# A deep attention layer whose rotary products are taken from PSUM by DVE, with POOL adding them and the FFN's next front a third earlier

## The chip, the cores and the metric

The kernel runs as one program on one core of a Trainium2 chip (trn2). The time is device time in microseconds, from the start to the end of an execution; several executions are given by their median. The engines are PE (TensorE), DVE (VectorE), ACT (ScalarE), POOL (GpSimd) and SP (SyncE, which only issues DMAs here).

## What is computed

Sixteen sequences of 256 rows with 128 channels go through four residual stages with layer norms. The change concerns the last one, a stack of six layers, each with a local attention and an FFN. Cut to what matters:

```python
def attn_layer(x, Wqkv, qs, ksc, Wo):            # x: (16, 256, 128), 16 heads of 64
    q, k, v = split(x @ Wqkv, 3)
    q = l2norm(q) * qs; k = l2norm(k) * ksc      # norm per row and head
    q = q * cos * scale + rotate_half(q) * sin * scale
    k = k * cos / scale + rotate_half(k) * sin / scale
    out = local_attention(q, k, v)               # windows of 32 rows, each looks at itself and the one before
    return out @ Wo

def ffn_layer(x, g, bln, W1, b1, W2, b2):
    a, gate = split(layernorm(x, g, bln) @ W1 + b1, 2)
    return a * gelu(gate) @ W2 + b2

for i in range(6):
    x = attn_layer(shift_tokens(x), ...) + x
    x = ffn_layer(shift_tokens(x), ...) + x
```

## The kernel before

All rows lie in SBUF as `X` (128 partitions, 32 blocks of 128 rows). The deep stage is written as one instruction stream for each engine, with semaphores between them. A sequence `n` is two blocks (`k`). Its work is put into 16 steps by hand-written tables (`PROJ_STEPS`, `SINE_STEPS`, `NORM_STEPS` and so on); `heads(n)` runs steps 0 to 15 of sequence `n`, steps 16 to 29 of `n - 1`, and the projection steps -16 to -1 of `n + 2` beside them. On every engine a step's order is: the attention's part first (`attend`), then the projection of `n + 2`, then what is left of `n + 1`. The streams loop over pairs of sequences (`Fori`), with the first and last ones of a layer written out.

The projection of a sequence has 13 slots: slot 0 turns the two blocks of X, slots 1 to 8 are the q and k products (k, part, half of 512 columns), slots 9 to 12 the four V products. A product is three matmuls (`split_product`, high and low parts). They go through two PSUM banks, `gen0` and `aux`, in turn. In the attention steps V slots of sequence `n + 1` stand between the q/k slots of `n + 2`: PE's order is slots 1, 2, 3, 4, V 9, V 10, 5, 6, 7, 8, V 11, V 12.

After a product, ACT copies the bank to `raw` (L1588) and squares it into `sq` (L1592), both inside the SBUF tile that the profile calls `spare`; then the bank is free (`proj_drained`). POOL multiplies the swapped halves by the sine table into `t2` (L1993, also `spare`), DVE multiplies `raw` by the cosine table in place (L1754), adds the two (L1761) and sums the squares per head (L1748). After the four quarters DVE works out the inverse norms by three Newton steps (L1767 to L1782), and POOL multiplies `raw` by them (L2003). PE turns the result (L1366), ACT keeps it in `qT` and `kT` (L1600).

The attention has two halves (`o`), each with scores (L1385, behind two mask matmuls L1376), maximum (L1804) and subtraction (L1810) on DVE, exponential on ACT, sum and reciprocal on DVE (L1817, L1819), normalisation of `E` on POOL (L2031), four sets of transposes per sequence (L1400), the product with V (L1419, "mix"), and at last the output product (L1431) and DVE's addition to X (L1824).

In the FFN a block of 512 rows has a front (turn, shift, turn back, statistics, normalise, turn: `f_in`, `f_return`, `f_norm` on PE, `f_shift`, `f_affine` on ACT, `f_stat`, `f_normal` on DVE) and a body of three hidden parts and an output (`f_hidden`, `f_output`). The front of the next block stands between the hidden parts. In all layers but the last, blocks 1 to 7 also carry the projections of the next layer's first two sequences (`prepare`), with the bank `gen0` alone (`single`).

Of the kernel before, what the change touches and what calls it, by code (L numbers as in the profile page):

```python
# [15 lines left out]
P = 128  # L16
D = 128
NBLK = 32
NSEQ = 16
# [1023 lines left out]
PROJ = 13  # L1043
TURN = 8
# [45 lines left out]
def slot_qkv(k, part):  # L1090

    return 1 + PROJ_ORDER.index((k, part, 1))
# [8 lines left out]
def deep_stage(nc, X, c, w, kept, raw):  # L1101
    with ExitStack() as ctx:
# [108 lines left out]
        proj_drained = sem("proj_drained")  # L1211
# [5 lines left out]
        cos_part = sem("cos_part")  # L1217
        sin_part = sem("sin_part")
# [39 lines left out]
        def _(sp):  # L1258
# [31 lines left out]
            def move_v(n, par, tail=False):  # L1290

                sp.wait_ge(proj_drained, count(slot_index(n, PROJ - 1, False, tail) + 1))
# [9 lines left out]
            def layer(l):  # L1302
                load_attn(l)
                move_v(l * NSEQ, 0)
                load_ffn(l)
                move_v(l * NSEQ + 1, 1)
                with sp.Fori(1, NSEQ // 2 - 1) as i:
                    move_v(l * NSEQ + 2 * i, 0)
                    move_v(l * NSEQ + 2 * i + 1, 1)
                move_v(l * NSEQ + NSEQ - 2, 0)  # L1310
                move_v(l * NSEQ + NSEQ - 1, 1, True)
# [15 lines left out]
        def _(pe):  # L1327
# [6 lines left out]
            def project(n, par, step, single=False, head=False, tail=False):  # L1334
# [6 lines left out]
                at = slot_index(n, slot, head, tail)  # L1341
                pe.wait_ge(proj_drained, count(at if single or place < 2 else at - 1))
# [141 lines left out]
            def f_in(m):  # L1484
                pe.wait_ge(f_staged, count(m + 1))
# [82 lines left out]
        def _(act):  # L1568
            def project(n, par, step, single=False, first=False, head=False, tail=False):
# [9 lines left out]
                else:  # L1579
                    k, part, a = PROJ_ORDER[slot - 1]  # L1580
                    cols = slice(a * 512, a * 512 + 512)
                    if part == 2:
# [3 lines left out]
                        act.activation(V[:, k, cols], gen[:], ACT.Copy).then_inc(proj_drained, 1)  # L1586
                    else:
                        act.activation(raw[:, par, k, part, cols], gen[:], ACT.Copy)  # L1588
# [3 lines left out]
                        act.activation(sq[:, part, cols], gen[:], ACT.Square).then_inc(proj_drained, 1)  # L1592
# [105 lines left out]
            def feed(l, g, front, ahead):  # L1698
                m = 8 * l + g
                for t in range(3):  # L1700
                    f_gelus(m, t)
                    if front and t == 0:
                        f_shift(m + 1)
                    if front and t == 2:
                        f_affine(m + 1)
                    if ahead:
                        for step in beside_feed(g, t):
                            prepare(l + 1, step)

# [31 lines left out]
        def _(dve):  # L1741
# [3 lines left out]
            def reduce_sq(n, k, part, head):  # L1745
                j = 2 * k + part
                dve.wait_ge(proj_drained, count(slot_index(n, slot_qkv(k, part), head) + 1))
                dve.tensor_reduce(ss[:, j * H:(j + 1) * H], heads_of(sq[:, part]), AX.X, ALU.add).then_inc(reduced, 1)  # L1748

            def cosine(n, par, k, part):  # L1750
# [6 lines left out]
            def add_parts(n, par, k, part):  # L1757
                j = n * 4 + 2 * k + part
                dve.wait_ge(cos_part, count(j + 1))
                x = raw[:, par, k, part]  # L1760
                dve.tensor_tensor(x, x, t2[:, part], ALU.add).then_inc(summed, 1)  # L1761
# [23 lines left out]
            def project(n, par, step, head=False):  # L1785
# [3 lines left out]
                for j in range(4):  # L1789
                    k, part = divmod(j, 2)  # L1790
                    if step == REDUCE_STEPS[j]:
                        reduce_sq(n, k, part, head)
                    if step == COSINE_STEPS[j]:
                        cosine(n, par, k, part)
                    if step == ADD_STEPS[j]:
                        add_parts(n, par, k, part)
# [51 lines left out]
            def low_x(n, par):  # L1848
# [5 lines left out]
                                  xT_hi[64:128, par, 1:SEQ + 1].bitcast(F32), ALU.subtract).then_inc(proj_drained, 1)  # L1854

            def make_tables(l):

                dve.wait_ge(attn_w_in, (l + 1) * ATTN_W)
                dve.wait_ge(cos_part, count(l * NSEQ * 4))
                dve.wait_ge(sin_part, count(l * NSEQ * 8))  # L1860
# [10 lines left out]
            def prepare(l, step):  # L1871
                n = l * NSEQ
                project(n + 1, 1, step - STEPS)
                project(n, 0, step, head=True)
# [57 lines left out]
            def feed(l, g, front, ahead):  # L1932
                m = 8 * l + g
                for t in range(3):
                    f_gated(m, t)
                    if front and t == 1:
                        f_stat(m + 1)
                    if front and t == 2:
# [35 lines left out]
            for step in range(FIRST_STEP, STEPS):  # L1974
                prepare(0, step)
# [8 lines left out]
        def _(pool):  # L1984
            def sine(n, par, k, part, first, head):
                j = n * 4 + 2 * k + part
                pool.wait_ge(proj_drained, count(slot_index(n, slot_qkv(k, part), head) + 1))
                if not (first and k == 0):
# [244 lines left out]
```

## Time and profile before

| what | us |
|---|---|
| median of 3 runs | 6131.73 |
| lowest and highest | 6127.62, 6131.87 |
| the profiled execution, its own time | 6136.03 |
| its span, first to last instruction | 6134.2 |
| DVE, ACT, POOL, PE busy in it | 4298.2, 2838.3, 3353.0, 4713.8 |

Busy time is what an engine spent in instructions that do work; a matmul's recorded times overlap their neighbours'. "Idle before" an instruction or group is time in which its engine did nothing, with the releaser that ended it. The granted clock of TensorE is 1.00 at 2.4 GHz and 0.50 at 1.2 GHz; its mean over the span is 0.866.

### The profile page before, as it was taken

How to read it: one execution, taken by the hardware profiler on the slowest of the kernel's cores; microseconds unless marked ns; L12 is line 12 of the kernel's file. 1: busy time of each engine (PE TensorE's matmuls, PEld its weight loads, DVE VectorE, ACT ScalarE, POOL GpSimd, SP SyncE). 2: the span in 40 equal slices, each digit the busy share in tenths (PEclk: the TensorE clock that was granted, in tenths of full speed). 3: DMA queues.
4: the chain of work that ended last, by engine and by line, in shares of the span. 5: the costliest groups of instructions: out<-in, count | busy, mean ns of one | idle time of the engine just before them, and what ended most of it. 6: DMA issues, size and time to landing. Idle time of an engine off the chain costs nothing. (4 is left out here: it accounts for less than half of the span.)

```text
span 6134.2 us, 175865 instructions
## 1 busy us (share of the span) xinstructions
PE 4713.8 (77%) x70592; PEld 3658.9 (60%) x70592; DVE 4298.2 (70%) x6496; ACT 2838.3 (46%) x5349; POOL 3353.0 (55%) x1834
## 2 busy tenths in 40 slices
PE   4986999947887678885788866888668887678875
PEld 3664877745666456664566655666546665466664
DVE  4346999958886478873688836888358884588854
ACT  2552333315554355552455534555335554355542
POOL 0004666637775367762577725777347774367741
PEclk8897999968998789986899978999778997798887
DMA  1000000002222012220122211222102222022220
GB/s 29 0 0 19 1 0 0 0 32 57 54 54 65 4 45 54 54 62 20 38 57 56 56 28 31 54 54 54 41 18 54 54 54 55 7 52 53 54 60 22
DMA packets 151608, 229.83 MB, mean 37 GB/s; under 512 B 33038, under 2 KB 56460, under 8 KB 149900
## 3 DMA queue, kind: packets, MB, share of 16 engines
q1 hardware_dynamic: 150924, 219.36, 15.0%
q8 instruction: 594, 9.73, 0.7%
q14 instruction: 90, 0.74, 0.0%
HBM read 26.31 MB, written 4.19 MB: 5 GB/s over the span
## 5 line engine op out<-in xcount | busy, mean ns | idle before, releaser
L1993 POOL TENSOR_TENSOR spare<-raw,table 128x512 f32<-128x512 f32 x768 | 1318.7, 1743 | 296.5 <-ACT spare L1592 296.5
L2003 POOL TENSOR_TENSOR raw<-raw,rs 128x1024 f32<-128x1024 f32 x384 | 821.8, 2151 | 694.5 <-DVE rs L1782 694.5
L1761 DVE TENSOR_TENSOR raw<-raw,spare 128x1024 f32<-128x1024 f32 x384 | 795.8, 2072 | 13.2
L1754 DVE TENSOR_TENSOR raw<-raw,table 128x1024 f32<-128x1024 f32 x384 | 736.8, 1919 | 62.3 <-POOL spare L1993 57.8
L1400 PE MATMUL trn<-ident,E 128*128 128x128 f32 x1536 | 329.5, 353 | 475.2 <-POOL E L2031 353.7
L1804 DVE TENSOR_REDUCE mx<-sco 128x16 f32<-128x1024 f32 x192 | 235.1, 1225 | 533.9 <-PE sco L1385 533.8
L2031 POOL TENSOR_TENSOR E<-E,rden 128x1024 f32<-128x1024 f32 x192 | 447.3, 2330 | 258.2 <-DVE rden L1819 258.2
L1400 PEld LDWEIGHTS trn<-ident,E 128*128 128x128 f32 x1536 | 237.3, 182 | 550.2 <-issue 366.2
L1611 ACT ACTIVATE room<-trn 128x512 f32<-128x512 f32 x384 | 230.1, 599 | 580.5 <-PE trn L1400 580.1
L1366 PE MATMUL trn<-ident,raw 128*128 128x128 f32 x3072 | 484.7, 281 | 9.2 <-ACT kT L1600 3.8
L1748 DVE TENSOR_REDUCE ss<-spare 128x16 f32<-128x1024 f32 x384 | 464.1, 1209 | 16.5 <-ACT spare L1592 16.4
L1419 PE MATMUL acc<-room,Vw 64*64 64x32 f32 x24576 | 449.4, 223 | 3.5 <-issue 3.5
L1366 PEld LDWEIGHTS trn<-ident,raw 128*128 128x128 f32 x3072 | 372.2, 143 | 126.3 <-ACT qT L1600 44.1
L1431 PE MATMUL wop<-wo,room 128*128 128x128 f32 x3072 | 409.7, 290 | 49.1 <-ACT room L1620 49.1
L1431 PEld LDWEIGHTS wop<-wo,room 128*128 128x128 f32 x3072 | 388.1, 203 | 67.2 <-ACT room L1620 51.1
L1419 PEld LDWEIGHTS acc<-room,Vw 64*64 64x64 f32 x24576 | 405.9, 138 | 35.7 <-issue 6.3
L1385 PEld LDWEIGHTS sco<-kT,qT 64*32 64x32 f32 x24576 | 265.5, 118 | 234.7 <-issue 234.1
L1385 PE MATMUL sco<-kT,qT 64*32 64x64 f32 (+1 forms) x24576 | 388.7, 241 | 20.7 <-issue 20.6
L1330 PE MATMUL gen<-wqkv_lo,xT_hi 128*128 128x512 f32 x636 | 339.2, 533 | 76.5 <-ACT spare L1592 53.5
L2072 POOL TENSOR_TENSOR rstd<-ve,half 128x4 f32<-128x4 f32 x48 | 48.9, 1019 | 622.6 <-DVE ve L1903 622.6
L1588 ACT ACTIVATE raw<-gen 128x512 f32<-128x512 f32 x432 | 261.1, 604 | 205.3 <-PE gen L1332 198.2
L1600 ACT ACTIVATE qT<-trn 128x512 f32<-128x512 f32 x384 | 232.7, 606 | 205.8 <-PE trn L1366 205.8
(220 smaller groups left out, 11388.7 us busy)
## 6 DMA issues: line engine op xcount, KB each, us to landing
Vw<-V SPq DMA_DIRECT2D x1344, 128.0 KB
Vw<-V SPq DMA_DIRECT2D x192, 64.0 KB
spare<-in_L_ffn_Wqkv SPq DMA_DIRECT2D x6, 1536.0 KB, 6.6
wo<-in_L_ffn_Wo SPq DMA_DIRECT2D x6, 512.0 KB, 3.9
X<-in_L_attn_x SPq DMA_DIRECT2D x16, 128.0 KB, 2.6
x_before_deep<-X SPq DMA_DIRECT2D x1, 2048.0 KB, 8.3
raw<-x_before_deep SPq DMA_DIRECT2D x1, 2048.0 KB, 8.0
out<-X SPq DMA_DIRECT2D x16, 128.0 KB, 2.0
```

The lines of the kernel that those rows point to most:

```text
L1330: pe.matmul(to, a_hi, b_lo, start=True, stop=False)
L1366: t = pe.transpose(trn[:, r * P:(r + 1) * P], raw[:, par, k, part, at:at + P], c["ident"][:])
L1385: t = pe.matmul(sco[g * WIN:g * WIN + WIN, hp, at:at + back + WIN], qT[lo:lo + 64, r, q:q + WIN], kT[lo:lo + 64, r, q - back:q + WIN], sta ...
L1400: t = pe.transpose(trn[:, i * P:(i + 1) * P], e[:, 4 * jj + i], c["ident"][:])
L1419: t = pe.matmul(acc[hp][64 * jp:64 * jp + 64, at:at + WIN], Vw[lo:lo + 64, par, k, g, (4 * o + j) * HD:(4 * o + j + 1) * HD], prT[lo:lo + ...
L1431: t = pe.matmul(wop[:, k * P:(k + 1) * P], oT[:, r, k * P:(k + 1) * P], wo[:, r], start=(r == 0), stop=(r == PAIRS - 1))
L1748: dve.tensor_reduce(ss[:, j * H:(j + 1) * H], heads_of(sq[:, part]), AX.X, ALU.add).then_inc(reduced, 1)
L1754: dve.tensor_tensor(x, x, table[:, part, 0, k][:, None, :].to_broadcast([P, H, HD]), ALU.mult).then_inc(cos_part, 1)
L1761: dve.tensor_tensor(x, x, t2[:, part], ALU.add).then_inc(summed, 1)
L1993: pool.tensor_tensor(dst[:, :, a], src[:, :, 1 - a], table[:, part, 1, k, 32 * a:32 * a + 32][:, None, :].to_broadcast([P, H, 32]), ALU.mu ...
L2003: pool.tensor_tensor(x, x, rs[:, at:at + H][:, :, None].to_broadcast([P, H, HD]), ALU.mult).then_inc(rotated, 1)
L2031: pool.tensor_tensor(E[:, o], E[:, o], rden[:, o][:, :, None].to_broadcast([P, ROWS, HD]), ALU.mult).then_inc(normed, 1)
```

## The change

The copy of q and k from PSUM by ACT falls away. DVE reads the projection's bank directly, three instructions per slot in the new `rope_parts`: the cosine product of 512 columns into `raw`, and two sine products of 8 runs of 32 columns each into `t2`. ACT's square is signalled on `squared`, and DVE starts a slot behind it. POOL, which multiplied before, now adds `raw` and `t2`. `proj_drained` is split: `qk_drained` is counted by DVE (the low part of X and the eight slots), `v_drained` by ACT (the four V slots), and the new `bank_free` gives the two counts that PE waits for before a slot. The step tables change with it, the Newton steps come one step earlier, and in the FFN each piece of the next block's front stands one hidden part earlier (`f_norm` stays behind the last of them).

```diff
-SINE_STEPS = (-11, -9, -5, -3)
-REDUCE_STEPS = (-11, -9, -5, -3)
-COSINE_STEPS = (-9, -7, -3, -1)
-ADD_STEPS = (-9, -7, -3, -1)
-NEWTON_STEP = -2
+ROPE_STEPS = (-13, -12, -11, -10, -8, -7, -6, -5)
+REDUCE_STEPS = (-12, -10, -7, -5)
+ADD_STEPS = (-11, -9, -6, -4)
+NEWTON_STEP = -3
...
+def bank_free(n, slot, single=False, head=False, tail=False):
+
+    i = slot - QK
+    if head and slot < QK:
+        return QK * n + slot, VS * n
+    if slot < QK:
+        if slot < 2 or single:
+            return QK * n + slot, VS * (n - 1) + (2 if slot >= 5 else 0)
+        if slot < 5:
+            return QK * n + slot - 1, VS * (n - 1)
+        return QK * n + max(slot - 1, 5), VS * (n - 1) + min(slot - 4, 2)
+    if tail:
+        return QK * (n + 1), VS * n + max(i - 1, 0)
+    if single:
+        return QK * (n + 1) + (5, 5, 9, 9)[i], VS * n + i
+    return QK * (n + 1) + (4, 5, 8, 9)[i], VS * n + (0, 0, 2, 2)[i]
...
-                at = slot_index(n, slot, head, tail)
-                pe.wait_ge(proj_drained, count(at if single or place < 2 else at - 1))
+                qk, v = bank_free(n, slot, single, head, tail)
+                pe.wait_ge(v_drained, count(v))
+                pe.wait_ge(qk_drained, count(qk))
...
             def feed(l, g, front, ahead):
                 m = 8 * l + g
+                if front:
+                    f_in(m + 1)
                 for t in range(3):
                     f_hidden(m, t)
-                    if front:
-                        (f_in, f_return, f_norm)[t](m + 1)
+                    if front and t == 0:
+                        f_return(m + 1)
                     if ahead:
                         for step in beside_feed(g, t):
                             prepare(l + 1, step)
+                if front:
+                    f_norm(m + 1)
                 f_output(m)
...
-                        act.activation(raw[:, par, k, part, cols], gen[:], ACT.Copy)
                         if a == 0 and not (first and k == 0):
 
                             act.wait_ge(reduced, count(n * 4 + 2 * k + part - 1))
-                        act.activation(sq[:, part, cols], gen[:], ACT.Square).then_inc(proj_drained, 1)
+                        act.activation(sq[:, part, cols], gen[:], ACT.Square).then_inc(squared, 1)
...
+            def rope_parts(n, par, slot, single, first, head):
+
+                k, part, a = PROJ_ORDER[slot - 1]
                 j = n * 4 + 2 * k + part
-                dve.wait_ge(sin_part, count(2 * j + 2))
-                x = heads_of(raw[:, par, k, part])
-                dve.tensor_tensor(x, x, table[:, part, 0, k][:, None, :].to_broadcast([P, H, HD]),
-                                  ALU.mult).then_inc(cos_part, 1)
...
+                gen = gen_of(slot_place(slot, head), single)
+                dve.wait_ge(squared, count(n * 8 + slot))
+                if a == 0 and not (first and k == 0):
+                    dve.wait_ge(summed, count(j - 1))
+                x, cols = heads_of(gen[:]), slice(a * 512, a * 512 + 512)
+                dve.tensor_tensor(heads_of(raw[:, par, k, part, cols]), x,
+                                  table[:, part, 0, k][:, None, :].to_broadcast([P, 8, HD]), ALU.mult)
+                src = gen[:].rearrange("p (h a d) -> p h a d", a=2, d=32)
+                dst = t2[:, part, cols].rearrange("p (h a d) -> p h a d", a=2, d=32)
+                for i in range(2):
+                    t = dve.tensor_tensor(dst[:, :, i], src[:, :, 1 - i],
+                                          table[:, part, 1, k, 32 * i:32 * i + 32][:, None, :].to_broadcast([P, 8, 32]),
+                                          ALU.mult)
+                t.then_inc(qk_drained, 1)
...
+            def add_parts(n, par, k, part):
+                j = 2 * k + part
+                pool.wait_ge(qk_drained, count(n * QK + 2 * j + 3))
+                x = raw[:, par, k, part]
+                pool.tensor_tensor(x, x, t2[:, part], ALU.add).then_inc(summed, 1)
```

DVE, between a sequence's first maximum (`mx<-sco`, a step 4) and the denominators of that half. Before:

```order
L1804 TENSOR_REDUCE mx<-sco 128x16 [waits scored]
L1807 ISA [waits maxed]
L1810 TENSOR_TENSOR E<-sco,mx 128x2x8x64 [waits p_turned]
L1747 ISA
L1748 TENSOR_REDUCE ss<-spare 128x16 [waits proj_drained]
L1817 TENSOR_REDUCE den<-E 128x16 [waits exped]
```

And now, from the slot in front of the maximum on (`raw<-aux,table` is the cosine product of a slot in bank `aux`, `spare<-aux,table` its two sine products):

```order
L1776 TENSOR_TENSOR raw<-aux,table 128x512 [waits summed]
L1781 TENSOR_TENSOR spare<-aux,table 128x8x32 x2
L1822 ISA
L1824 TENSOR_REDUCE mx<-sco 128x16 [waits scored]
L1827 ISA [waits maxed]
L1830 TENSOR_TENSOR E<-sco,mx 128x2x8x64 [waits p_turned]
L1772 REGISTER_ALU
L1776 TENSOR_TENSOR raw<-gen,table 128x512 [waits squared]
L1781 TENSOR_TENSOR spare<-gen,table 128x8x32 x2
L1765 TENSOR_REDUCE ss<-spare 128x16 [waits squared]
```

One slot now stands ahead of the maximum, and three more, with two reductions, behind it and ahead of the denominators.

DVE again, behind the second maximum of a sequence and its subtraction, from the addition to X on. Before:

```order
L1824 TENSOR_TENSOR X<-X,wop 128x256
L1752 ISA
L1754 TENSOR_TENSOR raw<-raw,table 128x1024 [waits sin_part]
L1759 REGISTER_ALU
L1761 TENSOR_TENSOR raw<-raw,spare 128x1024 [waits cos_part]
L1747 REGISTER_ALU
L1748 TENSOR_REDUCE ss<-spare 128x16 [waits proj_drained]
L1766 REGISTER_ALU
L1767 TENSOR_SCALAR hx<-ss 128x64 [waits reduced]
```

And now:

```order
L1844 TENSOR_TENSOR X<-X,wop 128x256
L1789 REGISTER_ALU
L1790 TENSOR_SCALAR hx<-ss 128x64 [waits reduced]
L1791 ISA
L1792 TENSOR_SCALAR seed<-hx 128x64 [waits newton]
```

The product, the addition and the reduction that stood between the addition to X and the inverse norms are gone from this place.

## Rows read from the trace of the kernel before

**Rows 1.** Ten steady sequences of layer 0: busy us of each engine and instructions.
```profile
1506.80:1882.00 375.20, 311.05 (x6376) 237.71 (x6375) 317.40 (x350) 215.42 (x400) 273.88 (x150) 0.91 0.24 55
```

**Rows 2.** The same stretch by line: busy us, mean ns, idle before.
```profile
L1993 POOL TENSOR_TENSOR spare<-raw,table 128x512 f32<-128x512 f32 x80 | 139.9, 1774 | 23.7 <-ACT spare L1592 23.7
L2003 POOL TENSOR_TENSOR raw<-raw,rs 128x1024 f32<-128x1024 f32 x40 | 85.5, 2146 | 78.5 <-DVE rs L1782 78.5
L1761 DVE TENSOR_TENSOR raw<-raw,spare 128x1024 f32<-128x1024 f32 x40 | 84.1, 2102 | 1.4
L1754 DVE TENSOR_TENSOR raw<-raw,table 128x1024 f32<-128x1024 f32 x40 | 76.8, 1919 | 0.5
```

**Rows 3.** DVE in one sequence: start us, us, instruction.
```profile
1732.59 0.41 DVE L1824 TENSOR_TENSOR X<-X,wop 128x256 f32 x1
1732.91 1.22 DVE L1754 TENSOR_TENSOR raw<-raw,table 128x1024 f32<-128x1024 f32 x1
...
1736.56 0.20 DVE L1767 TENSOR_SCALAR hx<-ss 128x64 f32<-128x64 f32 x1
...
1739.50 1.21 DVE L1817 TENSOR_REDUCE den<-E 128x16 f32<-128x1024 f32 x1
...
1745.40 0.41 DVE L1851 TENSOR_TENSOR xT_lo<-gen,xT_hi 64x256 fp32r<-64x256 f32 x1
...
1749.38 1.23 DVE L1804 TENSOR_REDUCE mx<-sco 128x16 f32<-128x1024 f32 x1 [3.12 <-PE sco L1385]
1750.73 1.22 DVE L1810 TENSOR_TENSOR E<-sco,mx 128x1024 f32<-128x1024 f32 x1
1751.88 1.21 DVE L1748 TENSOR_REDUCE ss<-spare 128x16 f32<-128x1024 f32 x1
```

**Rows 4.** POOL in the same sequence, same columns.
```profile
1739.66 1.90 POOL L2003 TENSOR_TENSOR raw<-raw,rs 128x1024 f32<-128x1024 f32 x1 [7.80 <-DVE rs L1782]
1741.52 2.88 POOL L2031 TENSOR_TENSOR E<-E,rden 128x1024 f32<-128x1024 f32 x1
```

**Rows 5.** PE, a sequence with the loop's end, then one without.
```profile
1704.27 0.78 PE L1376 MATMUL sco<-mask,identb 128*128 128x512 bf16 x2 [4.02 <-issue]
...
1707.17 1.11 PE L1400 MATMUL trn<-ident,E 128*128 128x128 f32 x4 [0.41 <-POOL E L2031]
...
1710.29 1.05 PE L1400 MATMUL trn<-ident,E 128*128 128x128 f32 x4
...
1744.62 1.11 PE L1400 MATMUL trn<-ident,E 128*128 128x128 f32 x4 [5.11 <-POOL E L2031]
...
1764.71 1.95 PE L1431 MATMUL wop<-wo,room 128*128 128x128 f32 x16
1766.49 0.60 PE L1400 MATMUL trn<-ident,E 128*128 128x128 f32 x4
1767.02 0.46 PE L1385 MATMUL sco<-kT,qT 64*32 64x32 f32 x32
```

**Rows 6.** PE at the full clock, the stretch after rows 5's first.
```profile
1718.00 0.18 PE L1411 MATMUL acc<-mask,identb 128*128 128x2 bf16 x1
...
1719.17 0.50 PE L1330 MATMUL aux<-wqkv_lo,xT_hi 128*128 128x512 f32 x1
...
1719.97 0.60 PE L1366 MATMUL trn<-ident,raw 128*128 128x128 f32 x4
1720.41 0.59 PE L1376 MATMUL sco<-mask,identb 128*128 128x512 bf16 x2
```

**Rows 7.** One stretch of windows: busy us as in rows 1, then PEclk.
```profile
1742.10:1748.90 6.80, 4.28 (x61) 3.02 (x69) 4.10 (x4) 1.50 (x3) 6.80 (x3) 0.50 0.67 152
```

**Rows 8.** By line over the whole run, shapes apart.
```profile
L1926 DVE TENSOR_TENSOR X<-X,aux 128x512 f32<-128x512 f32 x41 | 28.0, 684 | 130.1 <-PE aux L1525 130.1
```

**Rows 9.** Waits over the whole run: us in total, times, longest.
```profile
PE wop L1500 <- DVE room L1908: 207.4, 48, 12.9
...
PE sco L1376 <- issue: 115.4, 31, 4.6
```

More of the change, by code:

```diff
@@ L1043 @@
 PROJ = 13
+QK = 9
+VS = 4
 TURN = 8
@@ L1306, in layer @@
                 move_v(l * NSEQ + 1, 1)
[L1307 removed]
+                with sp.Fori(1, NSEQ // 2) as i:
                     move_v(l * NSEQ + 2 * i, 0)
                     move_v(l * NSEQ + 2 * i + 1, 1)
[L1310 to L1311 removed]
             layer(0)
@@ L1699, in feed @@
                 m = 8 * l + g
+                if front:
+                    f_shift(m + 1)
                 for t in range(3):
                     f_gelus(m, t)
[L1702 to L1705, printed above, removed]
                     if ahead:
@@ L1708, in feed @@
                             prepare(l + 1, step)
+                if front:
+                    f_affine(m + 1)
             def layer(l, last):
@@ L1783, in inverse, with project @@
                                              op0=ALU.add, op1=ALU.mult).then_inc(newton if i < 2 else inv_norm, 1)
-            def project(n, par, step, head=False):
+            def project(n, par, step, single=False, first=False, head=False):
                 if step == PROJ_STEPS[0]:
                     low_x(n, par)
[L1789 to L1796, printed above, removed]
+                if step in ROPE_STEPS:
+                    rope_parts(n, par, 1 + ROPE_STEPS.index(step), single, first, head)
+                if step in REDUCE_STEPS:
+                    j = REDUCE_STEPS.index(step)
+                    reduce_sq(n, j // 2, j % 2)
                 if step == NEWTON_STEP:
@@ L1935, in feed @@
                     f_gated(m, t)
+                    if front and t == 0:
+                        f_stat(m + 1)
                     if front and t == 1:
-                        f_stat(m + 1)
-                    if front and t == 2:
                         f_normal(m + 1)
@@ L1984, in _ @@
         def _(pool):
[L1985 to L1988, printed above, removed]
-                    pool.wait_ge(summed, count(j - 1))
-                src = raw[:, par, k, part].rearrange("p (h a d) -> p h a d", h=H, a=2)
-                dst = t2[:, part].rearrange("p (h a d) -> p h a d", h=H, a=2)
-                for a in range(2):
-                    pool.tensor_tensor(dst[:, :, a], src[:, :, 1 - a],
-                                       table[:, part, 1, k, 32 * a:32 * a + 32][:, None, :].to_broadcast([P, H, 32]),
-                                       ALU.mult).then_inc(sin_part, 1)
+            def add_parts(n, par, k, part):
[3 more added lines that the diff above has]
+                pool.tensor_tensor(x, x, t2[:, part], ALU.add).then_inc(summed, 1)
             def scale(n, par, k, part):
@@ L2015, in stage, with project @@
                     pool.tensor_copy(xs[:], X[:, bass.ds(2 * s, 2), :]).then_inc(staged, 1)
-            def project(l, s, par, step, first=False, head=False):
+            def project(l, s, par, step):
                 n = l * NSEQ + s
@@ L2022, in project @@
                 for j in range(4):
-                    if step == SINE_STEPS[j]:
-                        sine(n, par, j // 2, j % 2, first, head)
+                    if step == ADD_STEPS[j]:
+                        add_parts(n, par, j // 2, j % 2)
                     if step == SCALE_STEPS[j]:
@@ L2047, in heads, with prepare @@
                         project(l, s + 1, 1 - par, h)
-            def prepare(l, step, first=False):
+            def prepare(l, step):
                 project(l, 1, 1, step - STEPS)
-                project(l, 0, 0, step, first, head=True)
+                project(l, 0, 0, step)
             def low_wqkv(l):
@@ L2079, in prepare_beside @@
                     pool.wait_ge(f_added, count(8 * l + 1))
-                    pool.wait_ge(tables, count(l + 2))
                 for t in range(3):
@@ L2111, in _ @@
             low_wqkv(0)
-            pool.wait_ge(tables, count(1))
             for step in range(FIRST_STEP, STEPS):
-                prepare(0, step, True)
+                prepare(0, step)
             if DEPTH > 1:
```

37 lines of the change are left out of this document (14 added, 23 removed).

## The prediction

> **What bounds the kernel now.** I read first the busy shares of a steady stretch of the deep attention, then the costliest lines there, and then one sequence engine by engine, since no engine is full. In ten sequences of layer 0 PE is busy 311, DVE 317, POOL 274 and ACT 215 of 375 us [rows 1]: a sequence takes 37.5 us, and its length is that of a ring of waits. The reader is to see the ring in the next three groups. After the second maximum of a sequence DVE subtracts, adds to X, multiplies, adds and reduces, and only then computes the inverse norms (L1767 at 1736.56) and the denominators, which end at 1740.9 [rows 3]. POOL first scales one quarter of q and k (L2003) and then normalises E (L2031), 2.88 us long, until 1744.4 [rows 4]. PE has nothing left to do and waits 5.11 us for that; its transposes begin at 1744.62 and the second scores end at 1767.48 [rows 5]. So a sequence splits into 22.86 us from these transposes to the end of the second scores (call it B) and 14.69 us from there to the next transposes (call it A).
>
> Two further things matter. In every second sequence PE stands still for 4.02 us at the loop's end and waits for no other engine ("issue" [rows 5]; 31 times in the whole run [rows 9]), and in those E is only 0.41 us late. And at the end of the 5.11 us the granted clock of TensorE falls to 0.50 for 6.80 us [rows 7], the lower of its two levels, 1.2 against 2.4 GHz: four transposes then take 1.11 us instead of 0.60, 1.85 times as long (1744.62 and 1766.49 [rows 5]; at 1707.17, after the loop's end, the same 1.11).
>
> **The change part by part.** *DVE.* Per sequence it loses four multiplications of 1.92 us and four additions of 2.10 us (16.1 us [rows 2]) and gains 8 times three instructions that read PSUM. Their nearest rows: 0.684 us for 128x512 with one operand in PSUM [rows 8], 0.41 us for 128x256 (L1824), after which the next instruction begins 0.32 us later [rows 3]. I take 0.60 + 0.33 + 0.33 = 1.26 us for a slot; with no overlap it is 1.50; if a half with its runs of 32 elements cost as much as the full width, 0.60 + 2 x 0.60 = 1.80. The sum is 10.1 us per sequence, so DVE is relieved by 6 us. L1754 takes 1.22 us alone and 1.92 on the mean, since POOL's work lies over most of them; L1851, which reads PSUM, took 0.41 us although POOL was at work [rows 2 to 4]. I therefore give the new instructions no contention.
>
> The Trainium skill speaks against this: "VectorE: DVE Perf Modes", section "The DRAIN you can't avoid", says that a Vector instruction waits until the pipe of the one in front is empty, and its rules for authors ask for few instructions rather than few waits. The trace has successors that begin before the recorded end (1732.91 after 1732.59 + 0.41 [rows 3]). By the page a slot would be 1.50 us; the fourth of a microsecond between the two falls three times into a sequence's ring (below), and the sum would be 60 us higher, 6215.
>
> *POOL* loses eight products of 1.77 us (14.0 us) and gains four additions of 128x1024. The nearest rows are the scaling of the same size, 2.15 us, and two of the removed products, which have two full operands, 3.5 us [rows 2]. Even at 3.5 they are the 14 us that went; POOL isn't in the ring with them. Its scaling and E lose the contention: 1.90 us each instead of 1.90 and 2.88.
> *ACT* loses eight copies; it is busy 21.5 of 37.5 us [rows 1] and isn't in the ring.
> *The waits* are what I expect to decide. A projection bank is now free when DVE has multiplied, not when ACT has copied. DVE works in order, and between its first and second slot stands the maximum with its subtraction, then a reduction. PE's fourth q/k product waits for DVE's second slot and the V product behind it for the third, and everything else of PE is queued behind that: the two mixes, the remaining products, the second scores.
>
> A, new. DVE's reduction of the last quarter ends about 1.0 us after the scores (PE's eighth product ends 2.8 us before them, ACT and DVE follow in order). Then 1.35 + 1.15 for maximum and subtraction, 0.32 for X, 2.94 for the inverse norms (1736.56 to 1739.50 [rows 3]), POOL 0.26 + 1.86 + 1.90, PE 0.23: 11.0 us instead of 14.7. Gone from the way are multiplication, addition and reduction and E's contention. PE itself is ready after 9.6 us. In the sequences with the loop's end PE is the later one: 14.69 - 0.41, some 14.3 us; nothing is won there.
>
> B, new. Transposes, scores and first product 1.71 us at the full clock and 3.12 at the lower (1707.17 to 1710.29 [rows 5]); ACT 0.24 + 0.60 + 0.05; DVE's slot 1.26: 3.86 or 5.27 us. Then DVE: maximum and subtraction 2.50, slot 1.26, reduction 1.25, slot 1.26: 6.27 us, in which PE has one product, one set of transposes and another product, 2.0 us of work. Then PE without a break, by the rows of the full clock [rows 5, 6], each from its start to the next start: six products of 0.80, two mixes of 1.17, three sets of q/k transposes of 0.44, two of P of 0.53, masks of 0.5 and four scores of 0.4, one output product of 1.78: 13.4 us. B is 23.5 us at the full clock, 24.9 with the lower one at its start; before it was 22.9.
> In those 6.27 us PE is two thirds idle, in two pieces of 2.5 and 1.7 us. In the 5.11 us of before the clock fell [rows 5, 7]. I put it down as falling here too, and the loss as that of two products and one set of transposes (2.04 us of work at 1.85 times its length): 1.7 us, with 0 (the clock stays) and 2.4 (three products and the transposes) as bounds.
>
> So a sequence with free PE takes 11.0 + 23.5 + 1.7 = 36.2 us (1.3 less than now), one with the loop's end 14.3 + 24.9 + 1.7 = 40.9 us (3.4 more). In each layer 14 sequences run with projections beside them, 5 of them with the loop's end: 5 x 3.4 - 9 x 1.3 = +5.3 us, times 6 is +32 us.
>
> *FFN.* PE waits 207.4 us in 48 blocks for the normalised rows [rows 9]. The front now starts one third, six matmuls or 1.5 us, earlier in 7 of 8 blocks: at most 42 x 1.5 = 63 us. Against that, in the five layers in which the next layer is prepared beside the FFN only one bank is used, and 16 products per layer wait for DVE's 1.26 us instead of ACT's second pass of 0.49: at most 5 x 16 x 0.77 = 62 us. I let them cancel in five layers and keep 7 blocks x 1.5 = 10 us of gain in the last. Bounds: 63 gained, 62 lost. The removed waits for the tables and the split V waits cost nothing: they stand in front of work of later steps.
>
> Sum: 6136 (the profiled execution's own time, 4 us over the median of the runs) + 32 - 10 = 6158; against the median 6154. I say 6155.
>
> **The rivals.**
> *Faster: the clock stays up in the middle.* Then a sequence takes 34.5 or 39.2 us: 9 x 3.0 - 5 x 1.7 = 18.5 us per layer, 111 us in all, with the FFN's 10 us 6015 us; with the full clock after the loop's end too (1.4 us, 30 times) 5973. For it speaks that DVE and POOL lose 10 us of work between them per sequence and that A is shorter by 3.7 us; against it that B is longer and that PE idles in its middle. It is decided by whether DVE's second and third slot let PE's products through early enough that the granted clock stays at 1.00 between them.
> *The narrow products are dearer.* At 1.50 us a slot three of them in the ring add 0.7 us to 84 sequences, 60 us: 6215. At 1.80 they add 136 us: 6290. Nothing in the trace shows this shape on DVE, which is why it stays open.
> *The change moves nothing:* the ring stays what it was because POOL's E and PE's second half keep their distance; 5 slow and 9 quick sequences cancel, 6120 to 6145 us. For it: the two effects are of equal size and of opposite sign.
>
> **How the numbers follow.** The measurement tells 0.2%, 12 us, from no change. The likeliest case, PE paced by DVE with the clock falling, gets 0.42, its own range 6105 to 6230; faster through a clock that stays 0.31; dearer products 0.14; no effect 0.13. Faster by over 0.2% is then 0.31 and the lower edges of two others, 0.37; same 0.11; slower 0.52. The range goes from just above the lowest case to the upper end of the dear products: 5990 to 6290.
>
> **What would show it.** (1) DVE's slot of three at 1.26 us, with no longer times under POOL's work. (2) The transposes of E 11 us after the second scores in one sequence and 14 in the next; the 5.11 us idle gone or under 2. (3) PE idle in front of the fourth q/k product and the V product, released by DVE, and a clock of 0.50 there. (4) Steady sequences of 36 and 41 us in turn. (5) POOL's addition at 2.1 to 2.5 us with slack around it. Wrong if the clock doesn't fall there, if the pause at the loop's end shrinks, or if the sequences all get the same shorter length.

## The result, and the profile after

The changed kernel takes 6467.77 us (median of 4 runs, 6463.64 to 6493.60) where the kernel before takes 6131.8: ratio 1.056, interval 1.0535 to 1.0582. The profiled execution has a span of 6465.6 us, 331 us more than that of before. The forecast was 6155.

First the ten steady sequences of layer 0, then the middle of one of them: windows with busy us of PE, PEld, DVE, ACT and POOL, then PEclk, DMA share and GB/s, as in [rows 1].

```profile
1527.90:1956.10 428.20, 350.94 (x6381) 263.86 (x6380) 261.68 (x511) 185.50 (x321) 209.48 (x110) 0.82 0.21 48
1711.70:1725.40 13.70, 12.28 (x184) 9.19 (x183) 6.75 (x13) 4.07 (x7) 7.73 (x4) 0.51 0.01 2
```

Against [rows 1] DVE is relieved by 56 us and POOL by 64 us in ten sequences, as the counts of instructions promised, yet the ten take 53 us longer, and PE is busy 40 us longer with practically the same matmuls (6381 against 6376): the granted clock is 0.82 instead of 0.91. The same stretch by line, which answers to [rows 2]:

```profile
L2007 POOL TENSOR_TENSOR raw<-raw,spare 128x1024 f32<-128x1024 f32 x40 | 94.5, 2362 | 175.8 <-DVE spare L1781 175.8
L2015 POOL TENSOR_TENSOR raw<-raw,rs 128x1024 f32<-128x1024 f32 x40 | 75.7, 1902 | 42.9 <-DVE rs L1805 42.9
L1342 PE MATMUL gen<-wqkv_lo,xT_hi 128*128 128x512 f32 x60 | 34.3, 572 | 23.5 <-DVE spare L1781 23.5
L1776 DVE TENSOR_TENSOR raw<-gen,table 128x512 f32<-128x512 f32 x40 | 27.4, 686 | 23.5 <-ACT spare L1609 23.5
L1781 DVE TENSOR_TENSOR spare<-gen,table 128x256 f32<-128x256 f32 x80 | 29.8, 415 | 0.0
```

DVE in the middle of one sequence (timeline: start us, us, instruction, in brackets the idle time before it), to compare with [rows 3]:

```profile
1707.11 1.22 DVE L1824 TENSOR_REDUCE mx<-sco 128x16 f32<-128x1024 f32 x1
1708.46 1.23 DVE L1830 TENSOR_TENSOR E<-sco,mx 128x1024 f32<-128x1024 f32 x1
1709.60 0.68 DVE L1776 TENSOR_TENSOR raw<-gen,table 128x512 f32<-128x512 f32 x1
1710.20 0.74 DVE L1781 TENSOR_TENSOR spare<-gen,table 128x256 f32<-128x256 f32 x2
1710.86 1.21 DVE L1765 TENSOR_REDUCE ss<-spare 128x16 f32<-128x1024 f32 x1
1711.99 0.68 DVE L1776 TENSOR_TENSOR raw<-aux,table 128x512 f32<-128x512 f32 x1
```

And PE in the same sequence, against [rows 5, 6]:

```profile
1692.15 0.45 PE L1398 MATMUL sco<-kT,qT 64*32 64x32 f32 x32
...
1698.69 1.14 PE L1432 MATMUL acc<-room,Vw 64*64 64x32 f32 x64
...
1703.06 0.65 PE L1413 MATMUL trn<-ident,E 128*128 128x128 f32 x4 [0.99 <-POOL E L2043]
...
1707.25 0.50 PE L1342 MATMUL aux<-wqkv_lo,xT_hi 128*128 128x512 f32 x1 [0.54 <-DVE spare L1781]
...
1711.00 0.50 PE L1342 MATMUL gen<-wqkv_lo,xT_hi 128*128 128x512 f32 x1 [2.35 <-DVE spare L1781]
...
1713.39 0.80 PE L1342 MATMUL aux<-wqkv_lo,xT_hi 128*128 128x512 f32 x1 [1.43 <-DVE spare L1781]
...
1715.82 1.93 PE L1432 MATMUL acc<-room,Vw 64*64 64x32 f32 x64
...
1719.29 1.93 PE L1432 MATMUL acc<-room,Vw 64*64 64x32 f32 x64
...
1732.90 0.45 PE L1398 MATMUL sco<-kT,qT 64*32 64x32 f32 x32
```

The reader is to see two things. The 5.11 us in front of E's transposes have become 0.99, and A is 1703.06 - 1692.60 = 10.46 us. But in the middle PE waits three times for DVE's slot: 0.54 us, then 2.35 and 1.43 us with 1.0 us of product between them. The granted clock is at the lower level from 1711.7, between the last two waits, to 1725.4 (0.51 on the mean of the second window). PE works without a break from 1713.39 on, and it works slowly: a mix of 64 matmuls takes 1.93 us instead of 1.14. B is 1733.35 - 1703.06 = 30.3 us. Of the 66 steady sequences (eleven in each layer) 65 have a low clock that begins in the middle: 41 for 13.7 us, 7 for 10.2 us and 17 for only 3.4 or 6.8 us. Among those without the loop's end the ten with 6.8 us last 37.2 us, the 25 with 13.7 us 40.7. Steady sequences last 37 to 41 and 42 to 48 us in turn (mean 39.7 and 45.4); before they lasted 37.6 and 38.0.

From here on the time between DVE's additions to X tells where the 331 us are (each the difference to before, six layers or five gaps together): deep attention, from a layer's first to its last addition, +296; FFN, from the first to the last block's addition, -10; from an attention's end to the first block -18; from the FFN to the next layer's first addition +45; ahead of the first layer's first addition +19.

### The profile page after: what moved, and what is told of

Read it like the earlier page. It is cut to its first block and busy times, and to the rows that moved or that the text cites. A ratio compares the mean times of both kernels' runs of the same rounds, so it can differ in the third digit from the quotient of the medians.

```text
span 6465.6 us, 176300 instructions
## 1 busy us (share of the span) xinstructions
PE 5042.4 (78%) x70592; PEld 3854.8 (60%) x70592; DVE 3776.0 (58%) x8032; ACT 2542.2 (39%) x4581; POOL 2750.2 (43%) x1450
## 5 line engine op out<-in xcount | busy, mean ns | idle before, releaser
L2007 POOL TENSOR_TENSOR raw<-raw,spare 128x1024 f32<-128x1024 f32 x384 | 907.7, 2364 | 1594.4 <-DVE spare L1781 1594.4
L2015 POOL TENSOR_TENSOR raw<-raw,rs 128x1024 f32<-128x1024 f32 x384 | 727.5, 1906 | 378.3 <-DVE rs L1805 378.3
L1776 DVE TENSOR_TENSOR raw<-aux,table 128x512 f32<-128x512 f32 x336 | 230.6, 686 | 653.6 <-ACT spare L1609 653.6
L1432 PE MATMUL acc<-room,Vw 64*64 64x32 f32 x24576 | 554.8, 248 | 4.1 <-issue 3.9
L1609 ACT ACTIVATE spare<-gen 128x512 f32<-128x512 f32 x432 | 258.1, 597 | 702.8 <-PE gen L1344 702.8
L1432 PEld LDWEIGHTS acc<-room,Vw 64*64 64x64 f32 x24576 | 508.1, 167 | 43.6 <-issue 22.2
L1342 PEld LDWEIGHTS gen<-wqkv_lo,xT_hi 128*128 128x128 f32 x636 | 142.6, 224 | 544.3 <-DVE spare L1781 442.4
L1776 DVE TENSOR_TENSOR raw<-gen,table 128x512 f32<-128x512 f32 x432 | 296.7, 687 | 272.0 <-ACT spare L1609 271.7
L1342 PE MATMUL aux<-wqkv_lo,xT_hi 128*128 128x512 f32 x516 | 306.2, 593 | 146.7 <-DVE spare L1781 132.5
L1398 PE MATMUL sco<-kT,qT 64*32 64x64 f32 (+1 forms) x24576 | 381.8, 239 | 10.2 <-issue 10.0
L1609 ACT ACTIVATE spare<-aux 128x512 f32<-128x512 f32 x336 | 200.7, 597 | 407.5 <-PE aux L1344 407.5
```

The costliest lines, as they stand in the source:

```text
L1342: pe.matmul(to, a_hi, b_lo, start=True, stop=False)
L1398: t = pe.matmul(sco[g * WIN:g * WIN + WIN, hp, at:at + back + WIN], qT[lo:lo + 64, r, q:q + WIN], kT[lo:lo + 64, r, q - back:q + WIN], sta ...
L1432: t = pe.matmul(acc[hp][64 * jp:64 * jp + 64, at:at + WIN], Vw[lo:lo + 64, par, k, g, (4 * o + j) * HD:(4 * o + j + 1) * HD], prT[lo:lo + ...
L1776: dve.tensor_tensor(heads_of(raw[:, par, k, part, cols]), x, table[:, part, 0, k][:, None, :].to_broadcast([P, 8, HD]), ALU.mult)
L2007: pool.tensor_tensor(x, x, t2[:, part], ALU.add).then_inc(summed, 1)
L2015: pool.tensor_tensor(x, x, rs[:, at:at + H][:, :, None].to_broadcast([P, H, HD]), ALU.mult).then_inc(rotated, 1)
```

## Experiments

All are ratios to the kernel before, run on the same chip; "the changed kernel" is 1.056. The experiments are spread over three chips, on which the kernel before took 6130 to 6135 us, so a difference between two of them is good to some 5 us.

**1. Is it the clock?** Spare matmuls whose result nobody reads stand in PE's two middle waits. They add work and take no wait away.

```
+            def fill(n, times):
+                pe.wait_ge(head_out, count(4 * n - 2))
+                for _ in range(times):
+                    pe.matmul(acc[1][:], identb[:], mask[:], start=True, stop=True)
...
+                    if ahead >= 2 and not first and h == 5:
+                        fill(n, 5)
                     if ahead >= 1:
                         project(n + 1, 1 - par, h, tail=ahead == 1)
                         turn_qk(n + 1, 1 - par, h, among=True)
+                    if ahead >= 2 and not first and h == 4:
+                        fill(n, 10)
```

> The changed kernel, in which PE runs 10 and 5 spare 128x512 bf16 matmuls into the free bank acc[1] at the two places in the middle of a sequence where it waits for DVE (78 sequences); nothing of the result changes. In the changed kernel the granted clock is 0.50 for 13.7 us there, and from the V product to the end of the second scores PE takes 19.9 us where the rows at the full clock add up to 13.4. Theory A, the low clock is the cost: the clock stays at 1.00 in the middle, the 19.9 us become 13.5 to 14, a steady sequence takes 34.5 to 35.5 us (without the loop's end) and the kernel 5960 to 6060 us. Theory B, it is PE's wait for DVE's order alone and the clock only goes with it: DVE's rows don't move, the spare matmuls gain nothing, 6450 to 6500 us.

Measured: 6178.58 us, 1.0073 [1.0056, 1.009]. More work made the kernel 289 us faster. PE in the middle of a sequence of this kernel, and the window around it (nine of the ten spare matmuls are in the trace):

```profile
1675.94 0.65 PE L1413 MATMUL trn<-ident,E 128*128 128x128 f32 x4 [0.99 <-POOL E L2053]
...
1681.56 2.10 PE L1465 MATMUL acc<-mask,identb 128*128 128x512 bf16 x9
...
1683.87 0.49 PE L1342 MATMUL gen<-wqkv_lo,xT_hi 128*128 128x512 f32 x1 [0.20 <-DVE spare L1791]
...
1684.67 1.25 PE L1465 MATMUL acc<-mask,identb 128*128 128x512 bf16 x5
...
1686.25 0.50 PE L1342 MATMUL aux<-wqkv_lo,xT_hi 128*128 128x512 f32 x1 [0.33 <-DVE spare L1791]
...
1687.60 1.14 PE L1432 MATMUL acc<-room,Vw 64*64 64x32 f32 x64
...
1700.36 0.46 PE L1398 MATMUL sco<-kT,qT 64*32 64x32 f32 x32
```

```profile
1680.00:1694.00 14.00, 13.24 (x239) 8.72 (x241) 11.18 (x19) 6.42 (x12) 8.42 (x4) 1.00 0.24 56
```

The products start with the same distances to the transposes of E as in the changed kernel (7.9 and 10.3 us), for DVE still frees the banks when it did; only the clock stays at 1.00, the mixes take 1.14 us, and B is 24.9 instead of 30.3 us. The difference fits the clock alone: in the changed kernel PE works without a break at the low clock from 1713.4 to 1725.4, and at 1.85 times their length (the ratio of the transposes in the prediction) these 12.0 us are 6.5 us of work, 5.5 us lost; 5.4 are measured. Not one of the 66 steady sequences has a low clock in its middle. The 5960 to 6060 that theory A asked for were missed all the same: the sequences without the loop's end last 35.3 us, those with it 42.4.

**2. Can the wait itself be moved?** The first maximum stands two steps later, behind two more of DVE's slots, so that the 2.35 us wait goes.

```
-HIGHEST_STEPS = (4, 12)
-EXP_STEPS = (5, 13)
-TOTAL_STEPS = (7, 15)
+HIGHEST_STEPS = (6, 12)
+EXP_STEPS = (7, 13)
+TOTAL_STEPS = (8, 15)
```

> The changed kernel with the first maximum and subtraction of a sequence two steps later on DVE (step 6 instead of 4, exponential 7, sum 8), so that DVE's second and third slot stand ahead of it. PE's idle time before the V product falls from 3.8 to about 2.2 us in pieces, with 1.3 us more before the second V product; by the rows the middle is 0.9 us shorter. Theory A: if the clock stays up, 34 to 36 us per sequence and 5980 to 6080 us; if it still falls, 6350 to 6420 us. Theory B: only the 0.9 us in 84 sequences, 6390 us, whatever the clock does.

Measured: 6178.08 us, 1.0069 [1.0052, 1.0086]. This lies between the ranges of theory A (its clock stays up in some sequences and falls in others) and well under theory B's 6390, so the length follows the clock and not the waits alone. The 2.35 us wait is gone and the 1.43 us wait is left, and the clock falls in 26 of 66 sequences, in 23 of them for 10.2 us:

```profile
1687.00:1697.20 10.20, 9.96 (x178) 7.78 (x177) 6.65 (x11) 4.42 (x7) 5.35 (x3) 0.50 0.01 3
```

PE is busy for 98% of that window; it is the state it fell into that is slow, not its work. Where the clock doesn't fall a sequence without the loop's end lasts 34.5 us, the length that the rival "the clock stays up" had given; but this is the kernel with the later maximum. With the maximum where the change puts it, experiment 1 has 35.3.

**3. Both, and either wait alone.** The later maximum with five spare matmuls in front of the V product, and the changed kernel with the ten in the first wait only.

```
+                    if ahead >= 2 and not first and h == 5:
+                        fill(n, 5)
```

> The changed kernel with the first maximum two steps later, and five spare 128x512 matmuls (1.1 us) in front of the V product, where PE still waits 1.4 us. With the later maximum alone, layer 5 has no low clock in its middle and its sequences take 34.5 and 40.5 us (515.5 us), layers 0 to 4 lose 10.2 us to the low clock in many sequences and take 538 to 559 us. Theory A, the clock in the middle decides: layers 0 to 4 get layer 5's length, 5 x 30 us less than 6178: 6010 to 6060. Theory B, the layers differ by something else (a loop around them, DMA traffic) that shows itself as a wait too: 6160 to 6190.

> The changed kernel with only the ten spare matmuls in PE's first middle wait (2.35 us), and the second (1.4 us, in front of the V product) left. Theory A, each of the two waits can bring the clock down: as with the later maximum, whose 1.4 us were followed by 10.2 us of low clock in many sequences of layers 0 to 4; 10 to 40 us over the 6179 with both filled: 6190 to 6290. Theory B, the first wait alone does it: 6165 to 6185.

Measured: 6124.99 us, 0.998 [0.9969, 0.9991], and 6205.15 us, 1.0128 [1.0111, 1.0145]. The first misses its 6010 to 6060: the low clock is gone from the middle (1 sequence of 66), those without the loop's end last 34.5 us in every layer, but the others 41 to 43, where layer 5 has 38.8 to 40.7. Between its first and last addition to X, layer 5 was 34 us shorter than the mean of the others with the later maximum alone, and is 23 us shorter here. So only a third of that difference was the clock in the middle; some 10 us of what is left lie in the five sequences behind a loop's end, and the rest in the layer's last ones, where layer 5 is shorter in the kernel before too (24 against 34 us for one of them). The second median lies 27 us above the kernel with both spares, inside theory A's 6190 to 6290: the 1.4 us wait alone can bring the clock down. How often is open, for the profiled execution is the quickest of the four (6185 us) and has a fall in 6 of 66 sequences; the slower three were not profiled.

**4. What does PE's pause at the loop's end cost?** The kernel of experiment 1 with four sequences in PE's loop in place of two.

```
-                with pe.Fori(1, NSEQ // 2 - 1) as i:
-                    heads(n + 2 * i, 0)
-                    heads(n + 2 * i + 1, 1)
+                with pe.Fori(0, NSEQ // 4 - 1) as i:
+                    for s in range(2, 6):
+                        heads(n + 4 * i + s, s % 2)
```

> The changed kernel with the spare matmuls, and PE's loop over the deep sequences runs over four of them instead of two: two pauses at the loop's end per layer instead of five. In the trace of the kernel with the spare matmuls, sequences behind the loop's end last 42.3 us and the others 35.3. Theory A: the 7.0 us are the price of the pause (3.9 to 5.4 us, 1.0 to 1.6 inside the scores, and the low clock after it), and it goes with the jump: 3 x 7.0 us in 6 layers, 126 us less than 6179: 6040 to 6080. Theory B: the pause belongs to the length of the code that runs, not to the jump, and comes as often: 6165 to 6190.

Measured: 6032.82 us, 0.9833 [0.9816, 0.9849]: 146 us less, where A said 126, and just past A's range. Sequences inside the loop all last 35.3 to 36, those behind its end 39 to 43. One such end in the kernel of experiment 1:

```profile
1714.02 0.63 PE L1389 MATMUL sco<-mask,identb 128*128 128x512 bf16 x1 [5.37 <-issue]
1714.59 0.97 PE L1398 MATMUL sco<-kT,qT 64*32 64x32 f32 x51
1717.19 0.46 PE L1398 MATMUL sco<-kT,qT 64*32 64x64 f32 x13 [1.64 <-issue]
```

Behind 5.37 us a second pause of 1.64 us stands inside the scores, and the matmuls run at the low clock.

**5. The two halves of the change.** The rope part alone (the FFN as before), the front alone (the attention as before). The front's edit on PE, with ACT's and DVE's to match:

```
 def feed(l, g, front, ahead):
+    if front:
+        f_in(m + 1)
     for t in range(3):
         f_hidden(m, t)
-        if front:
-            (f_in, f_return, f_norm)[t](m + 1)
+        if front and t == 0:
+            f_return(m + 1)
...
+    if front:
+        f_norm(m + 1)
```

> The changed kernel with the FFN's front where it was before: only the rotary part of the change. The changed kernel's last FFN (without projections beside it) is 12 us shorter than before, and its other FFNs are as long as before, since the earlier front (some 5 to 8 us per layer) pays for products that wait for DVE in one bank. Expected: 6500 to 6530 us. If the front does nothing in the first five layers, 6480 us.

> The kernel before with only the FFN's front one third earlier. Expected: 12 us off in the last layer and 5 to 8 us in each of the other five, 6080 to 6095 us; if the front does nothing in the first five layers, 6120 us. The attention's sequences stay at 37.5 us.

Measured: 6563.23 us, 1.0684 [1.0663, 1.0706], and 5971.98 us, 0.9733 [0.9716, 0.9749]. Both left their range: the front is worth 162 us alone and 95 us beside the rope. PE's waits in the FFN of layer 0 (us in total, times, longest), first of before, then of the front alone:

```profile
PE wop L1500 <- DVE room L1908: 28.3, 6, 12.9
...
PE gen L1330 <- ACT spare L1592: 6.2, 6, 1.8
```

```profile
PE aux L1526 <- DVE room L1923: 13.3, 4, 5.8
...
PE wop L1501 <- DVE room L1913: 1.8, 2, 1.4
```

and of the changed kernel:

```profile
PE gen L1342 <- DVE spare L1781: 39.6, 14, 3.8
```

The front takes away 26.5 of 28.3 us of this waiting per layer, not 10.5; part of it comes back in front of the output product (L1526, 13.3 us, 6.3 before). The rope puts 39.6 us in their place, at the single bank that is used there. Over the FFN of each of the layers 0 to 4, this reads as 163 to 164 us before, 139 to 140 with the front alone, 167 to 170 with the rope alone, and 163 to 165 with both. So the bank's way over DVE costs only 3 to 7 us where PE waits for the front anyway, and over 20 where it doesn't.

**6. Is it that bank?** The changed kernel, but in the preparation beside the FFN ACT again copies the projection to raw and frees the bank; DVE makes both products from raw.

```
+                        if single:
+                            act.activation(raw[:, par, k, part, cols], gen[:], ACT.Copy)
                         act.activation(sq[:, part, cols], gen[:], ACT.Square).then_inc(squared, 1)
...
+                own = raw[:, par, k, part, cols]
+                source = own if single else gen[:]
```

> The changed kernel, but for the first two sequences of each layer, which are prepared beside the FFN with one bank, ACT again copies the projection into raw and frees the bank by its square; DVE makes both products from raw. Theory A: that bank's longer way over DVE is what takes away the gain of the earlier front (24 us per layer in the kernel with the earlier front alone) and lengthens the start of the next layer (76 against 64 us): 24 to 32 us less in five layers and up to 10 at the start, from 6468 to 6300 to 6350, FFN blocks summing to 139 to 146 us instead of 163. Theory B: it is DVE's and ACT's new order beside the FFN and not the bank: 6440 to 6475.

Measured: 6293.94 us, 1.0246 [1.0223, 1.027]: 174 us less than the changed kernel, just past A's range. The windows of the FFN of layer 0, first of the changed kernel, then of this one:

```profile
2101.40:2264.70 163.30, 107.47 (x462) 80.33 (x460) 80.82 (x215) 51.33 (x90) 53.89 (x35) 0.76 0.03 6
```

```profile
2093.30:2220.90 127.60, 92.38 (x462) 72.58 (x460) 91.67 (x215) 57.95 (x106) 56.29 (x35) 0.85 0.03 7
```

36 us less per layer, with more work for DVE and ACT, and 15 of them are PE's own busy time at a clock of 0.85 instead of 0.76. The first addition to X of the whole attention, 19 us late in the changed kernel, comes 13 us earlier again. Why a bank that is 0.8 us longer in use costs so much is seen on DVE in the changed kernel:

```profile
2207.23 0.75 DVE L1936 SCALAR_TENSOR_TENSOR room<-acc,b,room 128x512 f32<-128x512 f32 x1 [3.93 <-PE acc L1344]
2207.90 1.36 DVE L1926 TENSOR_SCALAR room<-wop,mv,rstd 128x128 f32<-128x128 f32 x4
2209.17 0.68 DVE L1776 TENSOR_TENSOR raw<-gen,table 128x512 f32<-128x512 f32 x1
2209.77 0.75 DVE L1781 TENSOR_TENSOR spare<-gen,table 128x256 f32<-128x256 f32 x2
```

The bank's product is queued behind the FFN's own product and normalisation, and DVE had waited 3.93 us for these; PE, at 2210.57, then waited 3.38 us for the bank.

**7. The ring of before with its clock up.** The front alone with twenty spare matmuls in PE's 5.11 us wait for E in every second sequence (the others have the loop's end there), then the same with PE's loop over four.

```
+                    if h == 2 and par == 1 and not first and ahead >= 2:
+                        fill(n, 20)
```

> The kernel before with the earlier front alone, and twenty spare 128x512 matmuls (4.3 us) in the 5.11 us for which PE waits for E in every second sequence. Theory A: the 6.8 us of low clock that follow this wait cost about 3 us of the ring in each of 6 sequences of 6 layers, and go: 5972 - 108, 5850 to 5900. Theory B: the ring takes the 3 us up elsewhere (DVE or the loop's end become late instead), or the clock falls anyway: 5960 to 5985.

> The kernel before with the earlier front, the spare matmuls where PE waits for E, and PE's loop over four sequences. Its sequences with the loop's end last 38.7 us, the others 36.3. If each pause costs 2.4 us of the ring: 3 x 6 x 2.4 = 43 us less than 5933, 5880 to 5900. If the ring of before (DVE, POOL's E) gives it back: 5920 to 5940.

Measured: 5932.52 us, 0.9663 [0.9647, 0.9679], and 5934.30 us, 0.9681 [0.9665, 0.9697]. The clock is worth 39 us there and not 108, between the two theories: sequences of 36.3 and 38.7 us instead of 37.5. Taking the pause away gains nothing (its rival's case): the sequences that lose it have no spare matmuls, and PE waits as long for E there, with a low clock behind it:

```profile
1552.16 1.11 PE L1400 MATMUL trn<-ident,E 128*128 128x128 f32 x4 [5.48 <-POOL E L2044]
```

They last some 38.2 us, hardly less than the 38.7 with the pause. What its removal is worth with that wait filled too was not tried.

**8. The later maximum, the five spare matmuls, the loop over four and ACT's copy together**, and then PE's twelve steady sequences in a line without a loop.

> The changed kernel with the four edits together: first maximum two steps later, five spare matmuls in front of the V product, PE's loop over four sequences, and ACT's copy in the preparation beside the FFN. Theory, each cause stands by itself: 6033 (spare matmuls and loop over four) less 0.8 us in some 60 quick sequences (34.5 instead of 35.3) and less the 174 us of the preparation: 5790 to 5840. Rival, the causes overlap (the preparation's gain needs the slow clock, or the longer loop adds pauses where the maximum is later): 5880 to 5960.

> The kernel with the four edits, and PE's twelve steady sequences written out in a line, with no loop in a layer. If the pause belongs to the jump: the last two of each layer go, 2 x 6 x 6.5 us, 78 us less than the kernel with the four edits. If it belongs to the length of the code that runs: no change, within 15 us, or more pauses in other places.

Measured: 5822.93 us, 0.9504 [0.9488, 0.952], and 5742.84 us, 0.9369 [0.9353, 0.9384], the fastest here. Both fall in their range; 80 us for the last jumps, where 78 were expected. Ten steady sequences of layer 0 of the last kernel:

```profile
1501.10:1846.50 345.40, 304.48 (x6431) 228.38 (x6430) 262.66 (x512) 182.20 (x321) 210.86 (x110) 1.00 0.26 59
```

The 66 steady sequences last 34.4 to 34.9 us, and the clock is 1.00 in this stretch.

## Why the prediction was wrong

*The slot, A and POOL: right.* A slot is 1.26 us (1709.60 to 1710.86), with 0.686 and 0.415 us for its parts against 0.684 and 0.41 forecast, and no longer under POOL's work; the 1.50 us does not show that the prediction drew from the Trainium skill, "VectorE: DVE Perf Modes", section "The DRAIN you can't avoid". The same section says that a next instruction which is not held starts earlier, and the trace agrees with that part: each part here starts 0.08 us before the recorded end of the one in front. POOL's sum takes 2.36 us, its scaling and E 1.90. A is 10.46 us (forecast 11.0), and with the loop's end 14.4 to 15.8 in layers 0 to 4 and 12.8 to 13.9 in layer 5 (forecast 14.3).

*Where PE waits, and that the clock falls: right.* Both pieces of idle time, 2.5 and 1.7 us in the forecast, are there with 2.35 and 1.43, released by DVE's slots, and the clock falls.

*The loss by the low clock: this step failed.* The forecast put it "as that of two products and one set of transposes", 1.7 us and at most 2.4. It took the low clock to last as long as the pieces of idle time and the work between them. The traces of the changed kernel and of experiments 1 to 3 show that it mostly lasts 10.2 or 13.7 us (48 of 65 sequences) and so over a stretch in which PE no longer waits: V product, two mixes, products, transposes. B is 30.3 us with 13.7 us of it, 26.7 with 6.8 us, and 24.9 with the clock kept up in the same order of work (experiment 1), so the term is 5.4 us, not 1.7; the forecast's size fits only the ten sequences with 6.8 us, at 1.9 us. Over the kernel, keeping the clock up in the middle gives back 289 of the 336 us.

*B at the full clock: 23.5 forecast, 24.9 measured.* The last part, from the V product on, takes 14.6 instead of 13.4 us. Of this, 0.82 us is a wait for ACT's copy of the turned k, which the forecast had left out although the kernel before has it too:

```profile
1728.82 0.66 PE L1413 MATMUL trn<-ident,E 128*128 128x128 f32 x4 [0.82 <-ACT kT L1617]
```

*The loop's end: too small.* The forecast gave these sequences 39.2 us at the full clock in the middle. Experiment 2 has 40.9 on the mean where the clock stays up there, experiments 1 and 3 have 42.4 and 41.5. In B the low clock of the pause costs 1.7 us in experiment 1 (26.6 against 24.9; forecast 1.4). The rest lies in A: 14.8 to 17.6 us in experiment 1, with a second pause of 0.9 to 2.0 us inside the scores in all 30 of these sequences. In the changed kernel and in experiment 2 none has that second pause, so the kernels with spare matmuls overstate the term for the changed kernel. There the sequences with the loop's end last 5.6 us more than the others, where the forecast had 4.7. In the new ring nothing waits as long as PE, so each pause counts in full: 6.4 us in experiment 2, 6.7 and 8.1 us per jump taken away in experiments 8 and 4. In the kernel before, sequences with and without it differ by some 0.1 us once a layer is under way (layers 0 to 4).

*The FFN: the right sum of two wrong terms.* Measured is -10 us in all, as forecast. But "one third, six matmuls or 1.5 us" is a third of a block of the last layer alone; in the other five layers the steps of the preparation stand in each third, and the front alone gives 23 to 25 us per layer instead of at most 10.5. The bank beside it costs as much (23 to 27 us against the front alone): "16 products times 0.77 us" left out that DVE's queue holds the FFN's own waiting instructions ahead of the slot (experiment 6).

*The starts of the attention: missing.* The preparation ahead of the first layer takes 19 us more, and the stretches from an FFN's end to the next layer's first addition 45 us more in five; the forecast had no term for either. Of the 19 us the bank's edit (experiment 6) gives 13 back. Of the 45 us it gives back only 6, the spare matmuls (experiment 1) 22 and the later maximum (experiment 2) 24, so the bank is the smaller part there; some 22 us stay even with the four edits together, and their cause is open.

*The sides.* The likelier direction was the right one, by the mechanism named, and the rival's price was near: with the clock up a sequence takes 35.3 us, where it said 34.5. That experiments 2, 3 and 8 have exactly 34.5 is luck, for they move the maximum, which the forecast did not.

## What to carry to other kernels

Price a new wait on TensorE not by its own length but by the work that follows it at the low clock: here 2.35 and 1.43 us of waiting were followed by a low clock that cost 5.4 us more in most sequences, and cheap spare matmuls in the wait gave them back. When a consumer takes over the freeing of a buffer, look at what is queued ahead of it on its engine in each place where the buffer is used, not only at how long its instruction takes. And a pause that hides in one ring (the loop's end) is paid in full once the ring is shorter than it, so a change that shortens a ring has to be tried together with the loop's form.

## What the hardware showed beyond that

The granted clock stayed at 0.50 for 13.7 us although PE was busy for 12.3 of them. PE pauses 3.1 to 5.6 us where its loop over two or four deep sequences jumps back, and not at all where the same instructions stand in a line. In experiment 1 all 30 of these pauses are followed by 0.9 to 2.0 us more inside the next scores, in the changed kernel and with the later maximum alone none; why is not known. On POOL a sum of two full operands of 128x1024 takes 2.36 us, a product with a broadcast operand 1.90. DVE's instructions on PSUM kept their 0.686 and 0.415 us beside POOL's work.
